# Another order of the steps of a pass in a software-pipelined attention and FFN kernel

## What is computed

```python
x = x + _layernorm(_L0_attn_ref(_layernorm(x), ...))   # one full causal attention, 16 heads of 8
x = x + _layernorm(_L0_ffn_ref(_layernorm(x), ...))    # 6 layers of windowed attention and FFN

def _L0_ffn_ref(x, ...):
    for i in range(DEPTH):                              # DEPTH = 6
        x = attn_layer(shift_tokens(x), Wqkv[i], q_scale[i], k_scale[i], Wo[i]) + x
        x = ffn_layer(shift_tokens(x), ln_g[i], ln_b[i], W1[i], b1[i], W2[i], b2[i]) + x
    return x
```

## Time and profile before

| | us |
|---|---|
| median of 3 runs | 2174.64 |
| lowest and highest of the runs | 2171.32, 2902.53 |
| profiled execution | 2173.78 |
| its span, first to last instruction | 2172.1 |
| project 0 of the first unit (start of the layer loop) | 337.3 |
| project 0 of the last unit | 1987.7 |
| end of the last new | 2150.3 |

### The profile page before, as it was taken

How to read it: one execution, slowest core, us unless ns; L and a number is a source line. 1 busy time by engine, 2 the same in 40 slices (tenths; PEclk the granted TensorE clock), 3 DMA queues, 4 the chain that set the end, 5 groups by cost and what they waited for, 6 DMA issues and landing times.

```text
span 2172.1 us, 46645 instructions
## 1 busy us (share of the span) xinstructions
PE 1842.0 (85%) x19848; PEld 798.9 (37%) x19848; DVE 1672.5 (77%) x2643; ACT 847.3 (39%) x1340; POOL 1100.6 (51%) x822
## 2 busy tenths in 40 slices
PE   5999946889989998898889898998998889888974
PEld 2333422334334433343334343333433344333431
DVE  5555556878897889878987888889788987888834
ACT  2344412433443344334443443344344433443420
...
GB/s 56 79 11 11 1 1 78 92 57 45 102 79 60 50 79 107 52 61 76 79 60 74 73 84 57 52 112 65 62 57 83 89 57 52 79 74 36 60 1 20
DMA packets 91749, 131.40 MB, mean 60 GB/s; under 512 B 16242, under 2 KB 35856, under 8 KB 91536
## 3 DMA queue, kind: packets, MB, share of 16 engines
...
## 4 chain that ended last, share of the span: by engine, by line
PE 45%; DVE 32%; POOL 12%; issue 5%; ACT 3%; DMA 2%; SPq 1%; POOLq 0%; DVEq 0%; ACTq 0%
PE ps_z L1078 11%; DVE t L740 7%; PE ps_s L1055 5%; PE ps_r L1000 4%; POOL prob L503 4%; POOL k_hat L489 3%; PE ps_r L1106 3%; PE ps_r L1109 3%; DVE sinv L771 3%; PE ps_r L1113 3%; DVE prob L764 2%; DVE t L660 2%; DMA t<-t 2%; PE ps_z L889 2%; DVE pt L777 2%
## 5 line engine op out<-in xcount | busy, mean ns | idle before, releaser
L1000 PE MATMUL ps_r<-xs,w_qk_sb 128*128 128x512 f32 x768 | 438.4, 660 | 139.7 <-ACT sq L555 96.7
L740 DVE TENSOR_TENSOR t<-ps_r,rot 128x1024 f32<-128x1024 f32 x384 | 456.7, 1208 | 45.7 <-PE ps_r L1000 41.0
L493 POOL TENSOR_TENSOR prob<-prob,top 128x1024 f32<-128x1024 f32 x96 | 182.7, 1903 | 485.5 <-DVE top L768 485.2
L555 ACT ACTIVATE sq<-ps_r 128x512 f32<-128x512 f32 x384 | 229.7, 598 | 428.9 <-DVE t L740 427.2
L1078 PE MATMUL ps_z<-z,vo 128*128 128x512 f32 x768 | 356.3, 607 | 2.2 <-ACT z L577 2.2
L489 POOL TENSOR_TENSOR q_hat<-t 128x512 f32<-128x512 f32 x192 | 241.9, 1276 | 189.0 <-DMA t<-t 188.5
L489 POOL TENSOR_TENSOR k_hat<-t 128x512 f32<-128x512 f32 x192 | 244.5, 1289 | 31.3 <-DMA t<-t 28.2
L1000 PEld LDWEIGHTS ps_r<-xs,w_qk_sb 128*128 128x128 f32 x768 | 120.3, 194 | 375.8 <-ACT sq L555 267.0
L577 ACT ACTIVATE z<-ps_z 128x512 f32<-128x512 f32 x384 | 214.2, 605 | 94.4 <-PE ps_z L1071 94.2
L1071 PE MATMUL ps_z<-pt,xtk 32*128 32x512 f32 x1536 | 203.3, 644 | 41.2 <-DVE pt L777 35.3
L761 DVE TENSOR_TENSOR k_hat<-k_hat,ps_s 128x1024 f32<-128x1024 f32 x96 | 117.2, 1221 | 112.8 <-PE ps_s L1035 112.7
...
## 6 DMA issues: line engine op xcount, KB each, us to landing
t<-t SPq DMA_DIRECT2D x768, 128.0 KB, 2.1
...
z<-q_hat SPq DMA_DIRECT2D x128, 16.0 KB
...
```

The costliest lines, as they stand in the source:

```text
L493: nc.gpsimd.tensor_tensor(s, s, top[:, (TT * u + n) % P_SLOTS, :].unsqueeze(2).to_broadcast([P, HEADS, 2 * WIN]), ALU.subtract).then_inc(l ...
L555: nc.scalar.activation(sq[:, n % SQ_SLOTS, :], ps_r[n % 2][:, :], ACT.Square).then_inc(squared.sem, 1)
L740: nc.vector.tensor_tensor(t12[:, slot, :, :], ps_r[n % 2][:, :].unsqueeze(1).to_broadcast([P, 2, SEQ]), rot[:, n // PAIRS, :, :], ALU.mult ...
L1000: nc.tensor.matmul(ps_r[n % 2][:, :], w_qk_sb[:, n, :], xs[:, seq, WIN:WIN + SEQ], start=True, stop=True).then_inc(projected.sem, 1)
```

## The change

The four tables are replaced. Each has the same steps as before with the same semaphores and banks; their order in a pass differs, and the place where the table is cut into passes too (`("out", 0, 2)` at the head of PE's table is now `("out", 0, 1)` near its end, which is the same place in the unrolled list). The table is a line shorter, so each line number of the kernel after is one less than before. Two lines of the difference:

```diff
-    ("hid", 2, 3), ("score", 1, 1), ("project", 0, 0), ("score", 2, 1), ("down", 0, 3), ("project", 1, 0),
+    ("hid", 2, 3), ("score", 1, 1), ("project", 0, 0), ("down", 0, 3), ("xturn", 1, 1), ("score", 2, 1),
...
-    ("gelu", 2, 3), ("square", 0, 0), ("exp", 0, 1), ("xcopy", 1, 1), ("square", 1, 0), ("exp", 1, 1), ("exp", 2, 1),
+    ("bias", 0, 3), ("gelu", 0, 3), ("vocopy", 0, 2), ("gelu", 1, 3), ("gelu", 2, 3), ("xcopy", 1, 1), ("exp", 0, 1),
```

More of the change, by code:

```diff
@@ L73 @@
 TENSOR_STEPS = [
-    ("out", 0, 2), ("project", 15, 1), ("nback", 0, 1), ("mean", 0, 3), ("xturn", 0, 1), ("spread", 0, 1),
-    ("sums", 3, 1), ("var", 0, 3), ("out", 1, 2), ("rows", 0, 3), ("spread", 1, 1), ("out", 2, 2), ("spread", 2, 1),
-    ("nturn", 1, 1), ("hid", 0, 3), ("spread", 3, 1), ("out", 3, 2), ("vo", 0, 2), ("hid", 1, 3), ("score", 0, 1),
-    ("hid", 2, 3), ("score", 1, 1), ("project", 0, 0), ("score", 2, 1), ("down", 0, 3), ("project", 1, 0),
-    ("xturn", 1, 1), ("project", 2, 0), ("score", 3, 1), ("project", 3, 0), ("mix", 0, 1), ("project", 4, 0),
@@ L79 @@
-    ("project", 5, 0), ("mix", 1, 1), ("project", 6, 0), ("project", 7, 0), ("sums", 0, 0), ("project", 8, 0),
-    ("project", 9, 0), ("mix", 2, 1), ("project", 10, 0), ("sums", 1, 0), ("project", 11, 0), ("nturn", 0, 0),
-    ("project", 12, 0), ("mix", 3, 1), ("project", 13, 0), ("project", 14, 0), ("sums", 2, 0),
+    ("sums", 3, 1), ("var", 0, 3), ("spread", 1, 1), ("out", 1, 2), ("rows", 0, 3), ("spread", 2, 1), ("out", 2, 2),
+    ("hid", 0, 3), ("nturn", 1, 1), ("spread", 3, 1), ("out", 3, 2), ("vo", 0, 2), ("hid", 1, 3), ("score", 0, 1),
@@ new lines @@
+    ("hid", 2, 3), ("score", 1, 1), ("project", 0, 0), ("down", 0, 3), ("xturn", 1, 1), ("score", 2, 1),
+    ("project", 1, 0), ("project", 2, 0), ("score", 3, 1), ("project", 3, 0), ("mix", 0, 1), ("project", 4, 0),
+    ("project", 5, 0), ("sums", 0, 0), ("project", 6, 0), ("project", 7, 0), ("mix", 1, 1), ("project", 8, 0),
+    ("project", 9, 0), ("project", 10, 0), ("mix", 2, 1), ("project", 11, 0), ("sums", 1, 0), ("project", 12, 0),
+    ("nturn", 0, 0), ("mix", 3, 1), ("project", 13, 0), ("project", 14, 0), ("sums", 2, 0), ("out", 0, 1),
@@ L82 @@
+    ("project", 15, 0), ("nback", 0, 0), ("mean", 0, 2), ("spread", 0, 0), ("xturn", 0, 0),
 ]
 VECTOR_STEPS = [
[L84 to L91, removed]
+    ("rotate", 12, 1), ("newton", 0, 1), ("rotate", 13, 1), ("rotate", 14, 1), ("rotate", 15, 1), ("center", 0, 3),
+    ("keyed", 0, 1), ("rstd", 0, 3), ("keyed", 1, 1), ("gain", 0, 3), ("keyed", 2, 1), ("keyed", 3, 1),
@@ new lines @@
+    ("gated", 0, 3), ("newton", 1, 1), ("gated", 1, 3), ("mask", 0, 1), ("max", 0, 1), ("gated", 2, 3),
+    ("mask", 1, 1), ("rotate", 0, 0), ("max", 1, 1), ("new", 0, 3), ("mask", 2, 1), ("psum", 0, 1), ("rotate", 1, 0),
+    ("max", 2, 1), ("x1", 0, 2), ("rotate", 2, 0), ("flip", 0, 1), ("psum", 1, 1), ("mask", 3, 1), ("rotate", 3, 0),
+    ("max", 3, 1), ("rotate", 4, 0), ("rotate", 5, 0), ("flip", 1, 1), ("rotate", 6, 0), ("psum", 2, 1),
+    ("rotate", 7, 0), ("rotate", 8, 0), ("flip", 2, 1), ("rotate", 9, 0), ("psum", 3, 1), ("rotate", 10, 0),
@@ L92 @@
+    ("rotate", 11, 0), ("flip", 3, 1),
 ]
 SCALAR_STEPS = [
-    ("zcopy", 15, 2), ("square", 13, 1), ("square", 14, 1), ("nrows", 0, 1), ("square", 15, 1), ("xsq", 0, 3),
-    ("nevac", 1, 1), ("bias", 0, 3), ("xcopy", 0, 1), ("gelu", 0, 3), ("vocopy", 0, 2), ("gelu", 1, 3),
-    ("gelu", 2, 3), ("square", 0, 0), ("exp", 0, 1), ("xcopy", 1, 1), ("square", 1, 0), ("exp", 1, 1), ("exp", 2, 1),
-    ("zcopy", 0, 1), ("square", 2, 0), ("zcopy", 1, 1), ("zcopy", 2, 1), ("square", 3, 0), ("zcopy", 3, 1),
@@ new lines @@
+    ("square", 0, 0), ("square", 1, 0), ("exp", 1, 1), ("zcopy", 0, 1), ("square", 2, 0), ("exp", 2, 1),
+    ("square", 3, 0), ("zcopy", 1, 1), ("zcopy", 2, 1), ("square", 4, 0), ("square", 5, 0), ("zcopy", 3, 1),
+    ("exp", 3, 1), ("square", 6, 0), ("zcopy", 4, 1), ("zcopy", 5, 1), ("square", 7, 0), ("zcopy", 6, 1),
+    ("square", 8, 0), ("zcopy", 7, 1), ("square", 9, 0), ("zcopy", 8, 1), ("zcopy", 9, 1), ("square", 10, 0),
+    ("zcopy", 10, 1), ("nevac", 0, 0), ("zcopy", 11, 1), ("square", 11, 0), ("square", 12, 0), ("zcopy", 12, 1),
@@ L102 @@
+    ("zcopy", 13, 1), ("zcopy", 14, 1), ("zcopy", 15, 1), ("square", 13, 0), ("square", 14, 0), ("nrows", 0, 0),
+    ("square", 15, 0), ("xsq", 0, 2), ("nevac", 1, 0), ("xcopy", 0, 0),
 ]
 GPSIMD_STEPS = [
-    ("add", 8, 3), ("add", 9, 3), ("add", 10, 3), ("add", 11, 3), ("add", 12, 3), ("add", 13, 3), ("add", 14, 3),
-    ("add", 15, 3), ("lower", 0, 3), ("scale", 0, 3), ("lower", 1, 3), ("scale", 1, 3), ("lower", 2, 3),
-    ("pnorm", 0, 3), ("scale", 2, 3), ("add", 0, 2), ("add", 1, 2), ("pnorm", 1, 3), ("add", 2, 2), ("lower", 3, 3),
@@ L107 @@
-    ("add", 3, 2), ("scale", 3, 3), ("pnorm", 2, 3), ("add", 4, 2), ("add", 5, 2), ("add", 6, 2), ("pnorm", 3, 3),
-    ("add", 7, 2),
+    ("add", 11, 3), ("add", 12, 3), ("add", 13, 3), ("add", 14, 3), ("add", 15, 3), ("lower", 0, 3), ("scale", 0, 3),
+    ("lower", 1, 3), ("scale", 1, 3), ("pnorm", 0, 3), ("add", 0, 2), ("lower", 2, 3), ("scale", 2, 3), ("add", 1, 2),
+    ("pnorm", 1, 3), ("add", 2, 2), ("lower", 3, 3), ("scale", 3, 3), ("add", 3, 2), ("add", 4, 2), ("pnorm", 2, 3),
+    ("add", 5, 2), ("add", 6, 2), ("add", 7, 2), ("pnorm", 3, 3), ("add", 8, 2), ("add", 9, 2), ("add", 10, 2),
```

## The result

The kernel after takes 2208.89 us (median of 4 runs, 2201.28 to 2227.69) against 2181.15 for the kernel before (median of 4): a ratio of 1.0177, with an interval of 1.0137 to 1.0217. The ratio leaves out one run of before that took 2902.53 us, which is also what lifts the median of its four; against the median of the other three, 2174.64, the median after is 1.0158, inside the interval. On the 2173.8 us of the profiled execution 1.0177 is +38 us where +11 was forecast. The sign holds, and so does the range (2208.89 lies in 2158 to 2212, near its end); 'within 2%' holds for the ratio, but the interval reaches beyond it; the size does not hold. (The interval is 0.4% to either side, finer than the 2% that the prediction took as about the limit.)

A forecast was written before the change was run, and what follows sets the result against it. A pass was taken as a head set by DVE and POOL together and a tail set by PE. 18 ordinary passes x 0.7 = +12.6 and 5 x -0.3 = -1.5 on 2173.8 gave 2185 us, range 2158 to 2212.

The forecast's parts named there:

- within 2%: Whole kernel: time after differs from before by no more than 2% (43 us), given a chance of 0.85.
- the clock is no term here: PE in the layer loop: granted 0.98 of its full clock, level of 2.4 GHz, so no time was counted for it.
- PE until project 15: PE from mix 0 (1055.1) to out 0's end (1084.2): wait before project 15 (1085.2) shrinks from 1.65 to about 1 us.
- PE stays off the chain: PE ahead of project 15: with about 1 us of cover left, PE does not set the pass time there.
- New and its 2.6 us earlier start: Head of the pass: down follows project 0, so new may start at 1043.88 in place of 1046.46, 2.58 us earlier.
- ACT's head as an edit that costs: ACT's head: exp 0 waits behind xcopy 1 and table load; psum 0 comes 1.2 us later than DVE alone could.
- The hole on POOL: POOL behind scale 1: pnorm 0 waits for psum 0 with its reciprocal, a hole of 1.4 us.
- The tail: PE from project 15 to the next project 0: same work without a hole, change 0, bounds -0.3 and +0.3 us.
- The passes that begin a layer: Five passes where DVE scales the rotary table: the hole ahead of new goes, -0.3 us each.
- Rival 1: Newton 0 on DVE meets one POOL add fewer: -0.4 us a pass, 2165 us in all; chance 0.24.
- Rival 2: On ACT, exp 3 waits for scale 3 and holds square 6: +1.7 us a pass, 2203 us; chance 0.18.
- Rival 3: ACT's table switch before exp 0 costs more than its row: psum 0 1.28 us later still, 2208 us; chance 0.05.

The follow-up runs named there:

- e1_fill: Kernel after plus 12 matmuls of a constant that nobody reads, in PE's idle stretch ahead of mix 0; 1.0062 of before.
- e1b_fill: e1_fill run once more, on the same chip as e9_fill_act; 1.0053 of before.
- e9_fill_act: e1_fill with the head of ACT in before's order (square 0, exp 0, xcopy 1); 1.0020 of before.

## Why the prediction was wrong in size, and what of it held

**The step that failed** is "the clock is no term here", and with it the step "PE until project 15". I read the clock off a window of before, 0.98, took it for a constant of the kernel, and put its term at nothing. It is a result of the order. The working had the rest: with my own numbers psum 0 starts at 7.4, rotate 1 ends at 9.9 and square 1 at 10.5, so project 3 ends near 11.6, and mix 0 starts at 15.1; 3.5 us of idle PE stood in that sum, and no price behind it. The words "PE stays off the chain" were then wrong too: for a few us behind mix 0 it is on it. Measured, a slow mix 0 adds 1.7 us to itself and moves rotate 4 from 19.23 to 20.85, and rotate 12 from 35.41 to 36.84 or, where the clock stays low for longer, to as much as 38.8. In mean passes it is 73.85 less 71.96, 1.9 us, beside a forecast of 0.7 in all; that is in the longest of the four runs, and by the ratios the clock costs 25 us, or 1.1 a pass.

The mean of 0.98 also hid that before loses its clock at times, which its own trace shows. Project 1 behind its wait for new, PE's timeline, and the window behind the second:

```profile
684.39 1.75 PE L1000 MATMUL ps_r<-xs,w_qk_sb 128*128 128x512 f32 x2 [1.61 <-DVE xs L812]
...
899.27 1.59 PE L1000 MATMUL ps_r<-xs,w_qk_sb 128*128 128x512 f32 x2 [3.72 <-DVE xs L812]
```

```profile
899.80:903.20 3.40, 3.40 (x8) 1.42 (x6) 3.13 (x5) 1.45 (x3) 3.40 (x3) 0.50 0.02 5
```

In the same 20 passes of before this wait is over 3 us three times (3.35, 3.72 and 3.07, where a layer begins), and project 1 is slow behind all three; it is 1.61 us in the other 17, and project 1 is slow in 4 of them (1.46 to 1.75 us in place of 1.12). A look at the rows behind waits of the length that the new order makes would have put a price on mix 0.

**The schedule itself held** once the clock is kept. Times in the ordinary pass shown of each kernel (from 1040.00 before, from 1043.80 in e1_fill, from 985.92 after):

| step | before | forecast | e1_fill | after |
|---|---|---|---|---|
| new | 6.46 | 3.9 | 3.75 | 3.74 |
| psum 0 | 8.0 | 7.4 | 7.18 | 7.18 |
| pnorm 0 | 9.59 | 8.98 | 8.76 | 8.77 |
| lower 3 | 19.27 | 20.15 | 20.01 | 20.0 |
| rotate 8 | 27.41 | 26.9 | 26.76 | 28.41 |
| rotate 12 | 34.53 | 35.45 | 35.41 | 36.84 |
| newton 0 | 35.67 | 36.6 | 36.53 | 37.95 |
| out 0 ends | 42.87 | 44.2 | 44.18 | 45.60 |
| project 15 | 44.52 | 45.2 | 45.28 | 46.41 |

Up to lower 3 after and e1_fill are one column; the steps behind the slow mix part them. These passes are a little shorter than most: the median of rotate 12 over the 14 is 34.82 before, 35.42 in e1_fill and 37.39 after. The forecast of +0.5% is what e1_fill (1.0062) and e1b_fill (1.0053) measure.

**Term by term.** New and its 2.6 us earlier start: right. ACT's head as an edit that costs: right, with 0.45 us in e9_fill_act. The working has psum 0 1.2 us later than DVE alone could, but its own mask 2 ends at 1046.95, 0.44 ahead of psum 0, which is what the run shows. The hole on POOL: right, forecast 1.4. After shows it here, with the table load and exp 0 ahead of it:

```profile
989.66 0.74 DVE L809 SCALAR_TENSOR_TENSOR xs<-ps_r,vec,x1s 64x512 f32<-64x512 f32 x1 [0.16 <-PE ps_r L1112]
990.72 1.28 ACT L571 ACT_TABLE_LOAD   x1
992.01 1.06 ACT L571 ACTIVATE prob<-prob 128x1024 f32<-128x1024 f32 x1
...
994.69 1.91 POOL L502 TENSOR_TENSOR prob<-prob,sinv 128x1024 f32<-128x1024 f32 x1 [1.22 <-DVE sinv L772]
...
1005.93 1.91 POOL L492 TENSOR_TENSOR prob<-prob,top 128x1024 f32<-128x1024 f32 x1
...
1023.87 0.21 DVE L751 TENSOR_SCALAR n_x<-ps_s 128x64 f32<-128x64 f32 x1
...
1032.33 1.12 PE L999 MATMUL ps_r<-xs,w_qk_sb 128*128 128x512 f32 x2 [0.81 <-ACT sq L554]
```

The cover of PE ahead of project 15 is 0.81, forecast about 1 (1.65 in the earlier trace rows). The tail is 26.6 us on the mean, as in before: 0 was right. The passes that begin a layer I had at -0.3; over five of them they are 77.94 on the mean before, 78.07 in e1_fill and 79.91 after. They scatter by up to 2.5 us in one trace, so a gain of 0.3 is not seen and not ruled out; taken as they stand, they are 0.43 off in each of five passes, 2 us of the 27 missed. Nearly all of the rest is the clock: 1.0177 less 1.0062 is 25 us.

**The rivals.** Rival 1 (one add fewer meets newton 0) did not happen in ordinary passes: newton 0 keeps its three held operations in all 14 of before, e1_fill and after, and from newton 0 to project 15 it is 8.73 us on the mean in before and in e1_fill, 8.56 in after. Where a layer begins it did: in the passes of units 8, 12 and 20 of e1_fill and after one of the three is gone, and the stretch is 7.80 to 7.97 us, where before has 8.61 to 8.78. Rival 2 (exp 3 holds square 6) fell: scale 3 ends at 23.9, as put, project 8 of e1_fill waits under 0.2 us in all but one pass, and e1_fill meets rotate 8. Rival 3 (a dearer table switch) fell: exp 0 begins 0.01 behind the load, as in the earlier trace rows. The time came out on rival 3's 2208 by chance, not by its mechanism. The range held by luck too, because it reached to rivals that did not happen.
